# First cross attention: two key chunks' value matmuls behind each other at every second step

## What is computed

```
qc = x @ w_q + b_q                       # 56 queries of one sequence
kc = ctx @ w_k + b_k                     # 1500 keys
vc = ctx @ w_v + b_v                     # 1500 values
scores = einsum('bhqd,bhkd->bhqk', heads(qc), heads(kc)) / sqrt(8)
attn = softmax(scores, axis=-1)
out = einsum('bhqk,bhkd->bhqd', attn, heads(vc))
x = layer_norm(x + out @ w_co + b_co, ln_g, ln_b)
```

## Time and profile before

| what | value |
|---|---|
| median of 3 runs | 1126.2 us (1124.32 to 1128.36) |
| the profiled execution, span | 1126.9 us (only the span is shown of this execution) |
| TensorE busy | 1046.1 us, 93% |
| VectorE busy | 759.8 us, 67% |
| ScalarE busy | 574.5 us, 51% |
| GpSimd busy | 389.9 us, 35% |
| first cross attention | about 119.5 to 488.6 us |
| mean granted clock of TensorE | 0.958 |

### The profile page before, as it was taken

How to read it: one execution, slowest core, us unless ns; L and a number is a source line. 1 busy time by engine, 2 the same in 40 slices (tenths; PEclk the granted TensorE clock), 3 DMA queues, 4 the chain that set the end, 5 groups by cost and what they waited for, 6 DMA issues and landing times. The chain is left out here.

```text
span 1126.9 us, 31634 instructions
## 1 busy us (share of the span) xinstructions
PE 1046.1 (93%) x12060; PEld 741.3 (66%) x12060; DVE 759.8 (67%) x1409; ACT 574.5 (51%) x1139; POOL 389.9 (35%) x273
## 2 busy tenths in 40 slices
PE   4977899999999998979596999999999999999997
PEld 2552566666666665655433777777777777777786
DVE  3646777888788878520575677667767777767652
ACT  2533567777677676642243444544444344444442
POOL 4822012111211112111102554545545555555542
PEclk8977889999999999979898999999999999999998
DMA  3501434344544443030002111111111110111100
GB/s 106 138 2 53 143 117 140 121 130 141 143 131 128 129 142 106 2 97 1 1 22 57 52 55 40 40 53 55 53 55 43 45 53 23 52 53 55 34 4 3
DMA packets 48462, 79.41 MB, mean 70 GB/s; under 512 B 8803, under 2 KB 35253, under 8 KB 48405
## 3 DMA queue, kind: packets, MB, share of 16 engines
q1 hardware_dynamic: 48404, 78.61, 23.1%
HBM read 51.13 MB, written 21.96 MB: 65 GB/s over the span
## 5 line engine op out<-in xcount | busy, mean ns | idle before, releaser
L1374 ACT ACTIVATE P<-PS 125x448 f32<-125x448 f32 x384 | 206.7, 543 | 270.7 <-PE PS L1283 268.7
L1264 POOL TENSOR_TENSOR Pl<-P 125x896 f16<-125x896 f32 x128 | 229.9, 1801 | 242.3 <-ACT P L1374 242.3
L1012 DVE TENSOR_REDUCE m<-PS 128x1 f32<-128x500 f32 x336 | 220.6, 674 | 120.2 <-PE PS L1003 118.4
L918 DVE TENSOR_REDUCE m_part<-PS 128x1 f32<-128x500 f32 x336 | 212.6, 674 | 59.6 <-PE PS L821 58.3
L896 ACT ACTIVATE Pb<-PS 125x448 f32<-125x448 f32 x384 | 187.9, 545 | 36.8 <-PE PS L796 36.1
L1299 PE MATMUL PS<-cNh,P 125*128 125x97 f16 x1344 | 198.1, 208 | 0.1
L1301 PE MATMUL PS<-cNh,Pl 125*128 125x97 f16 x1344 | 197.4, 207 | 0.0
L1300 PE MATMUL PS<-cNl,P 125*128 125x96 f16 x1344 | 196.9, 206 | 0.0
L1300 PEld LDWEIGHTS PS<-cNl,P 125*128 125x128 bf16 x1344 | 131.9, 98 | 25.5 <-issue 0.2
L1299 PEld LDWEIGHTS PS<-cNh,P 125*128 125x128 bf16 x1344 | 131.2, 98 | 15.8 <-issue 3.2
L1281 PE MATMUL PS<-Qh,cTh 110*125 110x448 f16 x384 | 139.0, 362 | 1.3 <-DVE Qh L1450 1.3
(11 more groups left out here) (170 smaller groups left out, 1555.5 us busy)
## 6 DMA issues: line engine op xcount, KB each, us to landing
Kst<-k_halves SPq DMA_DIRECT2D x144, 125.0 KB, 2.7
k_halves<-KH SPq DMA_DIRECT2D x16, 750.0 KB, 3.3
cx<-in_ctx SPq DMA_DIRECT2D x16, 562.5 KB
d_cx<-in_ctx SPq DMA_DIRECT2D x16, 562.5 KB
c_halves<-cHi SPq DMA_DIRECT2D x16, 281.2 KB, 2.7
c_halves<-cLo SPq DMA_DIRECT2D x16, 281.2 KB, 3.0
cTh<-c_halves SPq DMA_DIRECT2D x16, 281.2 KB, 2.9
cTl<-c_halves SPq DMA_DIRECT2D x16, 281.2 KB, 3.6
```

The costliest lines, as they stand in the source:

```text
L918: nc.vector.tensor_reduce(m_part[:, t, part:part + 1], PS[:, 6 + k % 2, 0:SP], AX.X, ALU.max).then_inc(s_reduced, 1)
L1012: nc.vector.tensor_reduce(m21[:, t, part:part + 1], PS[:, S1[k % 2], 0:SP], AX.X, ALU.max).then_inc(n_red, 1)
L1264: nc.gpsimd.tensor_tensor(Pl[:, c % NP], P1[:, c % NP], high, ALU.subtract).then_inc(n_low_p, 1)
L1374: nc.scalar.activation(P1[:, c % NP, half * HALF:(half + 1) * HALF], PS[0:KC, u % 3, 0:HALF], ACT.Exp).then_inc(n_exp, 1)
```

## The change

```diff
@@ -849,7 +849,8 @@
                             scores_t(i, par, c)
                         for k in pieces[:1]:
                             score_piece(i, par, k)
-                        if has_b and c >= LAG0:
+                        if has_b and c % 2 == 1 and c >= LAG0 + 1:
+                            values(i, par, c - LAG0 - 1)
                             values(i, par, c - LAG0)
 
                         if has_2 and not at_start and c < 3:
```

## The result

The changed kernel takes 1180.5 us (median of 4 runs, 1180.33 to 1183.44), the kernel before 1127.3 us beside it. The ratio is 1.0484, with a 95% interval of 1.0468 to 1.0501: 4.8% slower. 1190 was forecast, with a range of 1132 to 1206.

The account below looks back on a forecast made before the run. TensorE was taken to bound (busy 93%), VectorE pacing steps 1 to 3. Twelve bodies × (3.1 + 2.2) = 63.6, with +1.3, 0 and -1.3 elsewhere: +63.6 on 1126.9, 1190 us; range 1132 to 1206.

Parts of the forecast that it names:

- The start of GpSimd: End of a body: L772 starts 1.21 us behind P(20), ahead of mhigh and mneg by 0.13 to 0.33 us.
- The length of the wait: End of a body: VectorE blocked until GpSimd's run ends at 4.97; M at 5.3, or 5.1 if only L955 is blocked.
- wait and walk: Each body: M 3.3 us later, less 0.2 us gained in the rest of the body; growth of 3.1 us.
- The clock: Behind the wait at a body's end: TensorE's clock drops nearly each time, costing 0 to 2.8 us, taken as 2.2.
- Body 0, body 13, bodies 14 and 15: Bodies outside the twelve: +1.3 us in body 0, 0 in body 13, -1.3 in bodies 14 and 15 together.
- the first rival: Bodies' ends: VectorE blocked, but cheaper or dearer by the clock; 1163 to 1206 us, 70% with the sum.
- The rest of the body: Everything but a body's end: waits for VectorE leave 0.2 us gained per body; P(20) 0.18 us earlier.
- the 1.1 us: Each body on TensorE: eleven runs of V become six, sparing 5 × 0.22 us if nothing else bound.
- the fifth saving of 0.22: TensorE in each body: one of five savings of 0.22 us, each from a pairing sparing entering and leaving V.
- The second: Bodies' ends: GpSimd lets VectorE in ahead of L350, a body grows by 1.4 us; 1143 to 1170 us, 10%.
- The third: Bodies' ends: mhigh, L955 and L956 wait one GpSimd instruction each, +0.65 us a body; 1133 us, 9%.
- The fourth: Bodies' ends: nothing blocked; 1122.6 us (8%), or 1108.6 us if VectorE's pace did not bind either (2%).

Follow-up runs that it names:

- experiment 3: Changed kernel with 14 unused matmuls ahead of M in step 11, filling TensorE's wait: 1164.5 us (1.0338).
- the fifth pair alone: Kernel before with only V(8) moved from step 10 to stand with V(9) in step 11, the other V single: 1192.3 us (1.0567).
- experiment 1: GpSimd waits ahead of L772 until mneg is written: added to the changed kernel 1107.3 us (0.9837), to the kernel before 1110.1 us (0.9853).
- experiment 5: Kernels with GpSimd waiting for mneg, each reduction over 250 columns instead of 500: 1107.6 us (0.9838) without pairing, 1094.6 us (0.9726) with it.
- experiment 2's second run: Kernel before with only the first four pairs, in steps 3 to 9, and V(8) to V(11) singly: 1125.1 us (0.9984).

## Why the prediction was right

**The start of GpSimd.** Forecast at 1.21 us behind P(20) and ahead of both small instructions: 1.26 in even and 1.28 in odd bodies, 0.08 ahead of the cast. The second half of S(11) waited for the exponential as said. This decided the sign.

**The length of the wait.** M was forecast at 5.3, or at 5.1 if L955 alone is blocked: 5.16 and 5.19. The way there was a mixture of the two: the cast waited for one L772 (0.51), and `mneg` for all the rest. In body 0 it was the cast that waited for four L772 (1.98 us), and `mneg` for L350 (1.61). The growth of a body by wait and walk, 3.1 us forecast, was 2.9 (experiment 3): M came 3.15 us later in the mean instead of 3.3, and behind odd bodies M to S(0) had been 0.4 us longer (the 0.32 us that TensorE stands idle at S(0) of body 8, are in it). That is 0.24 us in experiment 3, and nothing in the changed kernel: the longer wait hides it.

**The clock, the term that was mis-sized.** 2.2 us a body forecast, 1.4 measured by experiment 3. For twelve bodies that is 10 us of the 14.6 by which their sum came out too high (63.6 forecast, 49.0 measured). The smaller growth is 2.9, and the 1.8 us that body 1 had lost to the clock before already, are the rest: I charged that body in full. It fell in all of bodies 1 to 12, and to 1.2 GHz, but it came back after 3.4 us, in time for S(0) (in the first of these bodies up to 0.4 us behind it): next to nothing was lost in the next body. I had it between 0 and the 2.8 of body 0, where it lasted 6.8 us. The run with the fifth pair alone shows that the longer fall happens behind the same wait, so this term depends on how wait and clock happen to meet.

**Body 0, body 13, bodies 14 and 15.** +1.3, 0 and -1.3 forecast; +2.2, +2.2 and 0.0 measured (-0.3 in body 14, +0.3 in the values of body 15). These give back 4.5 us of the 14.6, and 1.5 us less outside these sixteen bodies, of which the forecast had nothing, make up the span's 52.0: 49.0 + 4.5 - 1.5. Of these 1.5, 1.0 is S(0) of body 0, whose place differs from trace to trace (112.7 to 119.7 us); no V stands ahead of it. So the total is as near as it is partly by luck, since errors of both signs met in it. Body 14 gains nothing from the pairing: 20.15 us with it and 20.17 without in experiment 1. With the half reductions of experiment 5 it gains 0.7, so VectorE takes this gain too. Body 13's term was wrong in its working (the first rival had the longer wait, as the upper end of its times): I let `mneg` in between L678 and L680, but `mneg`'s second half had to wait for L680 too, as its timelines of VectorE and GpSimd show.

```profile
496.08 4.27 DVE L953 CAST mhigh<-mtop 128x7 f16<-128x7 f32 x1
...
500.40 2.35 POOL L680 TENSOR_TENSOR X<-X,rows 112x1024 f32<-112x1024 f32 x1
500.47 2.31 DVE L957 TENSOR_TENSOR mneg<-mhigh,mtop 128x7 f32<-128x7 f16 x1
```

**The rest of the body.** P(20) was forecast 0.18 us earlier and is 0.22 earlier. In step 2 (TensorE's timeline, body 8 after) T stands 0.25 us for the split and P(5) comes 1.22 us behind P(4), where the work between them costs 0.68:

```profile
342.37 0.38 PE L821 MATMUL PS<-KH,Qmx 128*128 128x500 f16 x1
343.00 0.63 PE L281 MATMUL PS<-tab,cx 125*96 125x125 f32 x4 [0.25 <-DVE cLo L332]
343.59 0.39 PE L821 MATMUL PS<-KH,Qmx 128*128 128x500 f16 x1
```

In the list of waits (waiter, waited for, us in total, times, longest) the pieces wait for VectorE's reductions 51 times instead of 19; the first row is of the changed kernel, the second of the kernel before:

```profile
PEld PS L821 <- DVE m_part L919: 20.7, 51, 1.1
```

```profile
PEld PS L821 <- DVE m_part L918: 10.5, 19, 1.1
```

That VectorE takes back 0.9 of the 1.1 us was argued from this; experiment 5 shows it for 0.6 of them (0.8 gained a body instead of 0.2). Of the 0.3 us that are left, most is the fifth saving of 0.22: it lies behind P(20), and from P(20) to S(0) of the next body it takes 3.9 us in even bodies with and without the pairing (experiment 1), so nothing is gained there. In front of M it is VectorE's chain that sets the time (1.84 us both times); behind M nothing was tried.

**The rivals.** The second (GpSimd lets VectorE in ahead of L350) happened in body 0 alone, and there for the cast only. The third (one instruction's wait each) held for the cast of bodies 1 to 12 (0.51 to 0.55 us) and not for `mneg`. The fourth, nothing blocked, is what experiment 2's second run shows when S(11) stays where it was.

## What to carry over

A small instruction on VectorE that TensorE waits for must not start behind a run of GpSimd, and who starts first may hang on 0.05 us: look in the timeline at what wakes GpSimd, and tie it to the end of the critical chain with a wait (here one wait, 16 us off the kernel before), instead of to an event that only happens to come later. A change to the order on one engine is read by what it releases on the others: the value matmuls saved TensorE what they were meant to, and a batch of V that leaves its place in front of the last scores woke GpSimd 0.33 us too early. A price for a drop of TensorE's clock that comes from one row should carry both of its lengths (3.4 and 6.8 us here).

## What the runs showed of the hardware

- An instruction of VectorE that meets running instructions of GpSimd was blocked for 0.42 to 0.55 us (to the end of one L772), 1.98 or 2.10 us (four), 3.16 us (three and L350) or 4.27 or 4.40 us (four and L678), always to within 0.04 us of an end on GpSimd. The Trainium skill, page "SBUF — State Buffer", section "Who interferes with whom", has the loser wait for the one instruction that holds the shared ports; the waits of 0.42 to 0.55 agree; in the others the end of that one instruction did not let VectorE in, and GpSimd went on with the next. There the measurement decides.
- What lets it in at a boundary was not settled. The kind of instruction on VectorE isn't it (3.15 us for a `tensor_tensor` with both inputs in SBUF, 3.16 for the `tensor_scalar`), nor is a satisfied wait ahead of GpSimd's instructions (1181.2 us). When L350 stood behind an unsatisfied wait, VectorE got in after one of the four L772; when L350 became free to follow just as VectorE began to wait, VectorE did not get in before L350's end. But with L350 free all along an instruction that began to wait during the first L772 still got in at its end: the cast of bodies 1 to 12 after the change (0.51 to 0.55 us) and L956 of the even bodies before it (0.55). Whether GpSimd's queue, its fetch or the lock decides this was not tried.
- The granted clock fell to 0.50 behind each wait of 3.16 us in front of M, and not once in bodies 1 to 12 when matmuls filled that wait. It stayed down for 3.4 us in the changed kernel (0.53 over the stretch shown above) and for 3.4 or 6.8 us with the fifth pair alone, behind waits of the same length.
